# A recommendation tower on one core: layer 1 in 6 chunks of rows in place of 8, with 28 pairs placed by small DMAs

## The chip, the cores and the metric

The kernel runs on one core of a Trainium2 chip. The metric is device time in microseconds (us) of one launch; it is taken as the median of several runs. A profile of one execution shows what each engine did: PE is TensorE, DVE is VectorE, ACT is ScalarE, POOL is GpSimd, SP is the engine that issues most of the DMAs.

## The reference

For 512 samples, 32 fields are looked up in 32 tables of 1000 to 12500 rows of 256 floats. The products of all pairs of fields i < j of a sample, with 16 dense values behind them, go through three layers.

```python
e = jnp.stack([tbl_0[ids[:, 0]], ..., tbl_31[ids[:, 31]]], axis=1)   # [512, 32, 256]
dots = jnp.einsum('bnd,bmd->bnm', e, e)
z = dots[:, iu, ju]                                                  # i < j: [512, 496]
h = jnp.concatenate([z, dense_ctx], axis=1)                          # [512, 512]
h = jnp.maximum(h @ W_top1 + b_top1, 0.0)                            # 512 wide
h = jnp.maximum(h @ W_top2 + b_top2, 0.0)                            # 256 wide
y = h @ W_top3                                                       # 1 wide
```

All of it is in float32.

## The kernel before

*Fields and samples.* Six fields with small tables are looked up by products with one-hot matrices on TensorE (the first third of the span), and the other 26 fields are gathered from HBM by indirect DMAs that POOL issues. There are 104 gathers, numbered 0 to 103, each of 128 rows (4 fields of 32 samples, or the last two fields of 64 samples). They go into a ring `rows` of 14 places; a gather waits until the gather 14 before it has been transposed (`transposed`), and for a point in the products (`dots_half_done`). Nothing else holds them.

*Fills.* TensorE transposes the gathered rows into one of three banks `xt_ps` (L580); that is a fill, of one or two gathers, and there are 57, numbered 0 to 56. ACT or DVE copies a fill into `xt` (L461 and L375; every third one from number 20 on, and number 56, are DVE's). Fill 38 is gather 71 alone. Fill 48 is gathers 89 and 90, fill 52 is gather 97, fills 53 and 54 are gathers 98 to 101, fill 55 is gather 102 and fill 56 is gather 103.

*Batches and rounds.* The 512 samples are 16 batches of 32, and four blocks of 128 (four batches each). `dots` (L608) computes the 32 x 32 products of a batch in 64 TensorE instructions into one of two banks. TensorE's order is written out by hand. After the lookups come rounds 0 to 14: round r computes the products of batch r, then the pieces of the layers that tables assign to the round (`LAYER2_IN`, `LAYER3_IN`, `LAYER1_IN`), then the fills of the round (`FILLS_IN`). Fill 48 is the last of round 12, fill 52 the last of round 13, and rounds 13 and 14 begin with products that need the fills of the round before. Round 14 has fills 53 to 56, and batch 15 comes behind it.

*Moves.* The products lie in a bank as four groups `s` of 32 partitions (row i of the products), with the samples and the column j in the free dimension. Layer 1 wants them with the rows of its contraction on 128 partitions. So `moves` (L255) copies for each `s` four quarters of 8 columns: columns 8q to 8q + 7 go to partitions 32q to 32q + 31 of `pairs`, whose chunk index is the column within the quarter. In quarter 0, chunk 0 would be column 0, which has no pair; the 16 dense values and the bias row lie there, loaded by `load_dense` (L284, on SP). DVE moves three of the four groups (L393), ACT one (L479), and two each in the last two batches. A move of a batch is thus 12 instructions on DVE and 4 on ACT, or 8 and 8.

*Layer 1.* For blocks 0 to 2, `layer1` (L614) contracts 8 chunks of 128 rows with `w1_sb`, for four groups of 128 outputs. `LAYER1_IN` splits the 8 half groups of a block over rounds. One product of 128x128x128 in float32 is two TensorE instructions in the profile, so a half group is 8 instructions and a block is 64. The last block is done per batch, to shorten the end: `flip(m)` (L641) computes the layer for the 32 samples of batch 12 + m with `pairs` as the weights (8 chunks x 4 quarters, 64 instructions), ACT or DVE copies it (`copy_flipped`), `turn(m)` (L651) transposes it, and `relu_turned` puts it into `h1`. Layer 2 is `layer2` (L668), layer 3 is L676.

*The end before.* In round 14, behind fill 54, stand flip 0, layer 2 of block 2, flip 1, turn 0, then fills 55 and 56, the products of batch 15, flips 2 and 3, layer 3 of block 2, turns 1 to 3, layer 2 and layer 3 of block 3, and the store of `y`. DVE applies the second relu of block 2 between its move of batch 14 and its copy of flip 1.

Of the kernel before, what the change touches and what calls it, by code (L numbers as in the profile page):

```python
# [13 lines left out]
P = 128  # L14
# [21 lines left out]
AT_ONCE = 2  # L36
JJ = N_FIELDS // QUADS
KEEP = 8
# [27 lines left out]
LAYER1_IN = {5: (0, [0, 1, 2]), 6: (0, [3, 4, 5]), 7: (0, [6, 7]), 9: (1, [0, 1, 2]), 10: (1, [3, 4, 5]),  # L66
             11: (1, [6, 7]), 12: (2, [0, 1]), 13: (2, [2, 3, 4]), 14: (2, [5, 6, 7])}
RELU1_IN = {7: 0, 11: 1, 14: 2}
# [7 lines left out]
def build_tower(nc, table, first_ids, ids, small_tables, small_ids, dense, w1, w2, b2, w3, out):  # L76
# [14 lines left out]
    with ExitStack() as ctx:  # L91
        def sb(name, shape, dt=F32):
            return ctx.enter_context(nc.sbuf_tensor(name, shape, dt))
# [25 lines left out]
        xt = sb("xt", [P, KEEP, DC, SAMPLES, N_FIELDS])  # L119
        pairs = sb("pairs", [P, 2, JJ, BLOCK])  # L120
        w1_sb = sb("w1_sb", [P, JJ, H1])
# [24 lines left out]
        small_ids_in = [sem(f"small_ids_in{k}") for k in range(TABLE_IDS)]  # L146
        no_pairs_zeroed = sem("no_pairs_zeroed")
        dense_in = [sem(f"dense_in{n}") for n in range(2)]
        w1_in = sem("w1_in")
# [101 lines left out]
        def round_of(f):  # L251

            return next(r for r in range(ROUNDS) if f in fills_in(r))

        def moves(n, s):  # L255

            b, at = divmod(n * SAMPLES, BLOCK)
            for q in range(QUADS):

                skip = int(q == 0)  # L260
                to = pairs[Q * q:Q * (q + 1), b % 2, skip:, at + s * GROUPS:at + (s + 1) * GROUPS]
                column = s % AT_ONCE * Q + q * JJ
                source = dots_ps[n % 2][Q * s:Q * (s + 1), :, column + skip:column + JJ]
                yield to, source.rearrange("i g j -> i j g")

# [15 lines left out]
        def _(sp):  # L281
            sp.dma_start(first_sb[:], first_ids).then_inc(first_ids_in, 16)

            def load_dense(b):  # L284
                sp.dma_start(pairs[0:dense.shape[0], b % 2, 0, :],
                             dense[:, b * BLOCK:(b + 1) * BLOCK]).then_inc(dense_in[b % 2], 16)
# [31 lines left out]
            sp.dma_start(w2_sb[:], w2).then_inc(w2_in, 16)  # L318
            for b in range(2, NB):

                sp.wait_ge(l1_done, N1 * (b - 1))
                load_dense(b)
            sp.wait_ge(y_ready, NB)
# [26 lines left out]
        def _(dve):  # L350

            nc.vector.memset(pairs[0:Q, :, 0, :], 0.0).then_inc(no_pairs_zeroed, 1)
            dve.wait_ge(first_ids_in, 16)
# [32 lines left out]
            def move(n):  # L386
                dve.wait_ge(dots_done, n + 1)
                if n % BATCHES == 0 and n // BATCHES >= 2:

                    dve.wait_ge(l1_done, N1 * (n // BATCHES - 1))  # L390
                for s in dve_quads(n):
                    for to, source in moves(n, s):
                        done = nc.vector.tensor_copy(to, source)  # L393
                done.then_inc(moved_dve, 1)
# [40 lines left out]
        def _(act):  # L435
# [36 lines left out]
            def move(n):  # L472
                act.wait_ge(dots_done, n + 1)
                if n % BATCHES == 0 and n // BATCHES >= 2:

                    act.wait_ge(l1_done, N1 * (n // BATCHES - 1))
                for s in act_quads(n):
# [38 lines left out]
            for r in range(ROUNDS):  # L516
# [11 lines left out]
                for f in fills_in(r):  # L528
# [15 lines left out]
        def _(pe):  # L544
# [67 lines left out]
            def layer1(b, n, columns, to):  # L612
                for j in columns:
                    done = nc.tensor.matmul(to, w1_sb[:, j, n * P:(n + 1) * P], pairs[:, b % 2, j, :],  # L614
                                            start=(j == 0), stop=(j == JJ - 1))
                if columns[-1] == JJ - 1:
                    done.then_inc(l1_done, 1)

            def pairs_complete(b):
                pe.wait_ge(moved_dve, BATCHES * (b + 1))  # L620
                pe.wait_ge(moved_act, BATCHES * (b + 1))
                pe.wait_ge(dense_in[b % 2], 16 * (b // 2 + 1))

            def flip(m):

                b = NB - 1
                moved = BATCHES * b + m + 1
                pe.wait_ge(moved_dve, moved)
                pe.wait_ge(moved_act, moved)
                if m == 0:  # L630
                    pe.wait_ge(dense_in[b % 2], 16 * (b // 2 + 1))

                    pe.wait_ge(h1_ready, b - 1)
                elif m == 1:
                    pe.wait_ge(h1_ready, b)
                elif m == 2:

                    pe.wait_ge(last_h1_act, 1)
                for j in range(JJ):
                    for q in range(QUADS):  # L640
                        done = nc.tensor.matmul(flip_ps[m][Q * q:Q * (q + 1), :],  # L641
                                                pairs[:, b % 2, j, m * SAMPLES:(m + 1) * SAMPLES],
                                                w1_sb[:, j, q * P:(q + 1) * P], start=(j == 0), stop=(j == JJ - 1))
                done.then_inc(flip_done, 1)
# [56 lines left out]
            for r in range(ROUNDS):  # L701
# [22 lines left out]
            layer3(NB - 2, l3_ps)  # L724
            for m in range(1, BATCHES):
                turn(m)

# [74 lines left out]
```

## Time and profile before

| | |
|---|---|
| median of three runs | 162.0 us (161.57 to 162.75) |
| profiled execution, its own time | 162.26 us |
| its span, first to last instruction | 160.5 us |
| granted TensorE clock, mean | 1.000 |
| busy: PE, weight loads, POOL, DVE, ACT | 148.6, 130.2, 104.0, 89.1, 73.0 us |
| instructions | 4781 |

The span is what the profile can divide; 1.76 us of the execution's time lie outside it. A busy TensorE is one with matmuls in flight, which overlap: an instruction of layer 1 is listed with 279 ns and one follows the other every 120 ns.

### The profile page before, as it was taken

How to read it: one execution, taken by the hardware profiler on the slowest of the kernel's cores; microseconds unless marked ns; L12 is line 12 of the kernel's file. 1: busy time of each engine (PE TensorE's matmuls, PEld its weight loads, DVE VectorE, ACT ScalarE, POOL GpSimd, SP SyncE). 2: the span in 40 equal slices, each digit the busy share in tenths (PEclk: the TensorE clock that was granted, in tenths of full speed). 3: DMA queues.
4: the chain of work that ended last, by engine and by line, in shares of the span. 5: the costliest groups of instructions: out<-in, count | busy, mean ns of one | idle time of the engine just before them, and what ended most of it. 6: DMA issues, size and time to landing. Idle time of an engine off the chain costs nothing.

```text
span 160.5 us, 4781 instructions
## 1 busy us (share of the span) xinstructions
PE 148.6 (93%) x1974; PEld 130.2 (81%) x1974; DVE 89.1 (56%) x287; ACT 73.0 (45%) x178; POOL 104.0 (65%) x110
## 2 busy tenths in 40 slices
PE   6999999899999989988989999799989798998994
PEld 6788888788868868777869989699979797997972
DVE  0799976746847034998708644708554344353410
ACT  3356787484764336564340543603441505071421
POOL 1587777777878777777777777777777777700000
PEclk9999999999999999999999999999999999999999
DMA  4899989778655756953333433343333333310000
GB/s 122 239 346 361 371 286 285 206 242 223 186 164 183 204 192 228 267 162 107 102 98 112 118 104 102 101 117 110 103 101 108 115 111 98 102 35 4 4 0 5
DMA packets 11423, 24.58 MB, mean 153 GB/s; under 512 B 2757, under 2 KB 3209, under 8 KB 11402
## 3 DMA queue, kind: packets, MB, share of 16 engines
q0 software_dynamic: 4992, 13.64, 29.2%
q1 hardware_dynamic: 6266, 10.38, 19.9%
q8 instruction: 16, 0.26, 0.6%
q10 hardware_dynamic: 144, 0.26, 0.6%
q14 instruction: 5, 0.04, 0.1%
HBM read 24.26 MB, written 0.00 MB: 151 GB/s over the span
## 4 chain that ended last, share of the span: by engine, by line
PE 40%; POOL 32%; issue 15%; DMA 9%; ACT 3%; DVE 0%; POOLq 0%
POOL rows L345 32%; PE bank L614 11%; PE bank L608 11%; DMA rows<-table,row_ids 6%; PE bank L641 5%; PE xt_ps L580 5%; PE bank L560 3%; PE bank L668 2%; DMA first_sb<-first_ids 2%; ACT xt L461 1%; PE xt_ps L668 1%; PE bank L676 1%; ACT h L495 0%; PE xt_ps L676 0%; ACT h L487 0%
## 5 line engine op out<-in xcount | busy, mean ns | idle before, releaser
L345 POOL DMA_INDIRECT rows<-table,row_ids x104 | 103.4, 994 | 35.0 <-issue 29.0
L393 DVE COPY pairs<-bank 32x64 f32<-32x64 f32 (+1 forms) x184 | 39.6, 215 | 6.7 <-PE bank L608 2.2
L461 ACT COPY xt<-xt_ps 128x512 f32<-128x512 f32 (+1 forms) x44 | 23.0, 557 | 36.3 <-PE xt_ps L580 35.8
L608 PE MATMUL bank<-xt 128*64 128x64 f32 x1024 | 33.4, 223 | 3.6 <-ACT xt L461 2.5
L608 PEld LDWEIGHTS bank<-xt 128*64 128x64 f32 x1024 | 31.3, 138 | 6.5 <-ACT xt L461 3.7
L580 PE MATMUL xt_ps<-ident,rows 128*128 128x128 f32 x208 | 29.6, 277 | 4.1 <-DMA rows<-table,row_ids 3.9
L580 PEld LDWEIGHTS xt_ps<-ident,rows 128*128 128x128 f32 x208 | 23.1, 140 | 8.5 <-DMA rows<-table,row_ids 4.2
L364 DVE TENSOR_SCALAR one_hot<-small_ids_sb,first_sb 128x512 fp32r<-128x512 int32 x48 | 22.2, 493 | 10.1 <-PE bank L560 10.1
L560 PE MATMUL bank<-one_hot,high 128*128 128x512 f32 x96 | 26.5, 398 | 0.0
L375 DVE COPY xt<-xt_ps 128x512 f32<-128x512 f32 (+1 forms) x13 | 8.2, 630 | 32.2 <-PE xt_ps L580 32.2
L560 PE MATMUL bank<-one_hot,low 128*128 128x512 f32 x96 | 25.8, 391 | 0.0
L614 PE MATMUL bank<-pairs,w_sb 128*128 128x128 f32 x192 | 23.7, 279 | 0.0
L614 PEld LDWEIGHTS bank<-pairs,w_sb 128*128 128x128 f32 x192 | 22.1, 192 | 0.9 <-issue 0.4
L560 PEld LDWEIGHTS bank<-one_hot,low 128*128 128x128 f32 x96 | 17.9, 188 | 4.0 <-DVE low L369 0.3
L560 PEld LDWEIGHTS bank<-one_hot,high 128*128 128x128 f32 x96 | 17.4, 188 | 3.8 <-DVE one_hot L364 0.4
L369 DVE TENSOR_TENSOR low<-small_sb,high 128x512 fp32r<-128x512 f32 x24 | 16.4, 683 | 0.4 <-ACT high L449 0.2
L449 ACT CAST high<-small_sb 128x512 fp32r<-128x512 f32 x23 | 13.9, 634 | 5.4 <-DMA small_sb<-small_tables 5.3
L456 ACT COPY kept<-bank 128x512 f32<-128x512 f32 x11 | 11.6, 1161 | 10.2 <-PE bank L560 10.2
L479 ACT COPY pairs<-bank 32x56 f32<-32x56 f32 (+1 forms) x72 | 14.6, 203 | 3.5 <-PE bank L608 2.5
L641 PE MATMUL bank<-w_sb,pairs 128*32 128x128 f32 x256 | 7.8, 274 | 0.0
L641 PEld LDWEIGHTS bank<-w_sb,pairs 128*32 128x32 f32 x256 | 6.7, 110 | 0.6 <-DVE pairs L393 0.3
L668 PE MATMUL bank<-h,w_sb 128*128 128x128 f32 x48 | 6.2, 281 | 0.0
(37 smaller groups left out, 41.3 us busy)
## 6 DMA issues: line engine op xcount, KB each, us to landing
small_sb<-small_tables SPq DMA_DIRECT2D x23, 256.0 KB, 5.1
w_sb<-w SPq DMA_DIRECT2D x8, 256.0 KB
rows<-table,row_ids POOLq DMA_INDIRECT x104, 3.7
small_ids_sb<-small_ids SPq DMA_DIRECT2D x5, 256.0 KB, 5.8
w_sb<-w SPq DMA_DIRECT2D x1, 512.0 KB, 5.9
small_ids_sb<-small_ids ACTq DMA_DIRECT2D x1, 256.0 KB, 3.7
small_sb<-small_tables SPq DMA_DIRECT2D x2, 128.0 KB, 3.5
ids_sb<-ids SPq DMA_DIRECT2D x1, 100.0 KB, 3.2
```

What stands on the lines that cost most here:

```text
L345: nc.gpsimd.indirect_dma_start(rows[:, i % ROWS, :], None, table, bass.IndirectOffsetOnAxis(ap=row_ids[:, i:i + 1], axis=0)).then_inc(gath ...
L364: nc.vector.tensor_scalar(one_hot[:, i % ONE_HOTS, :], small_ids_sb[:, k % TABLE_IDS, :], chunk_rows_sb[:, c:c + 1], None, ALU.is_equal).t ...
L369: nc.vector.tensor_tensor(low[:, k, c - 1:c + 1, :], small_sb[:, k, c - 1:c + 1, :], high[:, k, c - 1:c + 1, :], ALU.subtract).then_inc(lo ...
L393: done = nc.vector.tensor_copy(to, source)
L449: nc.scalar.copy(high[:, k, c:c + 2, :], small_sb[:, k, c:c + 2, :]).then_inc(high_ready, 1)
L461: nc.scalar.copy(*fill_parts(f)).then_inc(xt_act, 1)
L479: done = nc.scalar.copy(to, source)
L560: last = nc.tensor.matmul(banks[FOUND_BANKS[k][d]][:], part[:, k % TABLES, c, d * P:(d + 1) * P], one_hot[:, i % ONE_HOTS, :], start=(c == ...
L580: last = nc.tensor.transpose(to, rows[:, i % ROWS, c * P:(c + 1) * P], ident[:])
L608: done = nc.tensor.matmul(dots_ps[n % 2][quads, g, :], x, x, start=(c == 0), stop=(c == DC - 1))
L614: done = nc.tensor.matmul(to, w1_sb[:, j, n * P:(n + 1) * P], pairs[:, b % 2, j, :], start=(j == 0), stop=(j == JJ - 1))
L641: done = nc.tensor.matmul(flip_ps[m][Q * q:Q * (q + 1), :], pairs[:, b % 2, j, m * SAMPLES:(m + 1) * SAMPLES], w1_sb[:, j, q * P:(q + 1) * ...
```

## The change

Columns 0 to 7 are no longer a quarter of their own. The 24 columns 8 to 31 make four quarters of 6, so `pairs` has 6 chunks in place of 8 (`JJ`), and `w1_sb` too: 48 instructions of layer 1 for a block in place of 64, 48 for a flip in place of 64. Quarter 0 holds columns 8 to 13, whose pairs i < j need rows 0 to 12 only, and 14 rows are kept for them (`OWN_ROWS`). The 28 pairs of the first 8 fields (columns 1 to 7) go to rows 14 to 21 and 22 to 29 of quarter 0, which are free: `side_move` copies 14 rows x 13 columns (1 to 13) x 8 samples of each group in one instruction to `pairs`, 7 chunks of which (`SIDE`) are only a place to put them down, and then two DMAs from SP carry the columns 1 to 5 and 6 to 7 from partitions 0 to 7 to their rows. For blocks 0 to 2 that is one pair of DMAs for a block, for the last block one pair for a batch. Layer 1 of a block and each flip wait for them.

The number of copies stays 4 for each group: one of 14 partitions x 104 elements and three of 32 x 48, in place of one of 32 x 56 and three of 32 x 64. All side moves of a batch stand ahead of its other moves, on DVE and on ACT.

The order changes too: layer 1 of block 2 is done in rounds 13 and 14 (4 half groups of 6 instructions each) and not in round 12 any more; layer 2 of block 2 goes from between flips 0 and 1 to between flips 2 and 3, with turn 1 behind it; DVE's second relu of block 2 goes behind its copy of flip 2; ACT's relu of turn 1 goes ahead of its copy of flip 3. The zeroing at the start covers 32 x 1536 elements in place of 32 x 256, and SP loads 6 chunks of layer 1's weights in place of 8. The weights are laid out for it on the host.

```diff
+FIRST = 8
+SIDE = FIRST - 1
+JJ = (N_FIELDS - FIRST) // QUADS
+OWN_ROWS = FIRST + JJ
+
+SIDE_PLACES = (OWN_ROWS, 0, JJ - 1), (OWN_ROWS + FIRST, JJ - 1, SIDE)
-JJ = N_FIELDS // QUADS
...
-             11: (1, [6, 7]), 12: (2, [0, 1]), 13: (2, [2, 3, 4]), 14: (2, [5, 6, 7])}
+             11: (1, [6, 7]), 13: (2, [0, 1, 2, 3]), 14: (2, [4, 5, 6, 7])}
...
-        pairs = sb("pairs", [P, 2, JJ, BLOCK])
+        pairs = sb("pairs", [P, 2, SIDE + JJ, BLOCK])
+        own_pairs = pairs[:, :, SIDE:, :]
...
+        def side_move(n, s):
+            half, samples = places(n, s)
+            return pairs[0:OWN_ROWS, half, :, samples], source_of(n, s, OWN_ROWS, 1, SIDE + JJ)
+
         def moves(n, s):
-            b, at = divmod(n * SAMPLES, BLOCK)
-            for q in range(QUADS):
-                skip = int(q == 0)
-                to = pairs[Q * q:Q * (q + 1), b % 2, skip:, at + s * GROUPS:at + (s + 1) * GROUPS]
-                column = s % AT_ONCE * Q + q * JJ
-                source = dots_ps[n % 2][Q * s:Q * (s + 1), :, column + skip:column + JJ]
-                yield to, source.rearrange("i g j -> i j g")
+            half, samples = places(n, s)
+            for q in range(1, QUADS):
+                yield own_pairs[Q * q:Q * (q + 1), half, :, samples], source_of(n, s, Q, FIRST + q * JJ, JJ)
...
-            for b in range(2, NB):
-                sp.wait_ge(l1_done, N1 * (b - 1))
-                load_dense(b)
+            def place_sides(b, samples, into):
+                for row, first, last in SIDE_PLACES:
+                    sp.dma_start(own_pairs[row:row + FIRST, b % 2, 1:1 + last - first, samples],
+                                 pairs[0:FIRST, b % 2, first:last, samples]).then_inc(into, 16)
+            for b in range(NB):
+                if b >= 2:
+                    sp.wait_ge(l1_done, N1 * (b - 1))
+                    load_dense(b)
+                if b < NB - 1:
+                    sp.wait_ge(sides_moved_act, BATCHES * (b + 1))
+                    sp.wait_ge(sides_moved_dve, BATCHES * (b + 1))
+                    place_sides(b, slice(0, BLOCK), sides_in[b])
+            for m in range(BATCHES):
+                sp.wait_ge(sides_moved_act, BATCHES * (NB - 1) + m + 1)
+                sp.wait_ge(sides_moved_dve, BATCHES * (NB - 1) + m + 1)
+                place_sides(NB - 1, slice(m * SAMPLES, (m + 1) * SAMPLES), last_sides_in[m])
...
-            nc.vector.memset(pairs[0:Q, :, 0, :], 0.0).then_inc(no_pairs_zeroed, 1)
+            nc.vector.memset(own_pairs[0:Q], 0.0).then_inc(no_pairs_zeroed, 1)
...
+                for s in dve_quads(n):
+                    done = nc.vector.tensor_copy(*side_move(n, s))
+                done.then_inc(sides_moved_dve, 1)
...
                         move(NM - 2)
-                        dve.wait_ge(biases_in, 32)
-                        dve.wait_ge(l2_done, (NB - 1) * N2)
-                        for k in range(N2):
-                            nc.vector.tensor_scalar(h2[:, k, :], l2_ps[k], b2_sb[:, k:k + 1], 0.0,
-                                                    ALU.add, ALU.max).then_inc(h2_ready, 1)
                         copy_flipped(1)
...
             copy_flipped(2)
+            dve.wait_ge(biases_in, 32)
+            dve.wait_ge(l2_done, (NB - 1) * N2)
+            for k in range(N2):
+                nc.vector.tensor_scalar(h2[:, k, :], l2_ps[k], b2_sb[:, k:k + 1], 0.0,
+                                        ALU.add, ALU.max).then_inc(h2_ready, 1)
...
             move(NM - 1)
+            relu_turned(1)
             copy_flipped(3)
             keep_y(NB - 2, l3_ps)
-            relu_turned(1)
             relu_turned(3)
...
             def pairs_complete(b):
...
+                pe.wait_ge(sides_in[b], 16 * len(SIDE_PLACES))
             def flip(m):
...
+                pe.wait_ge(last_sides_in[m], 16 * len(SIDE_PLACES))
...
                         flip(0)
-                        layer2_of(NB - 2)
                         flip(1)
                         turn(0)
                     fill(f)
             for half in (2 * NM - 2, 2 * NM - 1):
                 dots(half)
             flip(2)
+            layer2_of(NB - 2)
+            turn(1)
             flip(3)
             layer3(NB - 2, l3_ps)
-            for m in range(1, BATCHES):
-                turn(m)
+            turn(2)
+            turn(3)
```

ACT has the same loop of side moves, with `sides_moved_act`, ahead of its own moves.

## Rows read from the trace of the kernel before

**Rows 1.** The page: busy time of PE and POOL, and the chain by line.
```profile
PE 148.6 (93%) x1974; PEld 130.2 (81%) x1974; DVE 89.1 (56%) x287; ACT 73.0 (45%) x178; POOL 104.0 (65%) x110
...
POOL rows L345 32%; PE bank L614 11%; PE bank L608 11%; DMA rows<-table,row_ids 6%; PE bank L641 5%; PE xt_ps L580 5%; PE bank L560 3%; PE bank L668 2%; DMA first_sb<-first_ids 2%; ACT xt L461 1%; PE xt_ps L668 1%; PE bank L676 1%; ACT h L495 0%; PE xt_ps L676 0%; ACT h L487 0%
```
**Rows 2.** Who waited for whom: POOL's gathers (total us, times, longest us).
```profile
POOL rows L345 <- issue: 29.0, 95, 0.3
```
**Rows 3.** Timeline of POOL: gathers 33, 97 and 103 (start us, us).
```profile
50.85 1.36 POOL L345 DMA_INDIRECT rows<-table,row_ids  x1 [0.30 <-issue]
...
131.39 0.95 POOL L345 DMA_INDIRECT rows<-table,row_ids  x1 [0.30 <-issue]
...
138.89 0.95 POOL L345 DMA_INDIRECT rows<-table,row_ids  x1 [0.30 <-issue]
```
**Rows 4.** The chain in order of time (start us, us, what).
```profile
98.87 2.74 DMA rows<-table,row_ids
...
101.74 0.41 PE xt_ps L580 x2
...
110.46 2.88 PE bank L614 x24
```
**Rows 5.** Timeline of PE, rounds 12 to 14 and the end.
```profile
123.76 1.95 PE L614 MATMUL bank<-pairs,w_sb 128*128 128x128 f32 x16
...
127.86 2.08 PE L608 MATMUL bank<-xt 128*64 128x64 f32 x64 [0.83 <-ACT xt L461]
...
133.18 1.71 PE L580 MATMUL xt_ps<-ident,rows 128*128 128x128 f32 x14
135.48 2.08 PE L608 MATMUL bank<-xt 128*64 128x64 f32 x64 [0.59 <-ACT xt L461]
...
141.25 1.96 PE L641 MATMUL bank<-w_sb,pairs 128*32 128x128 f32 x64
143.13 2.05 PE L668 MATMUL bank<-h,w_sb 128*128 128x128 f32 x16
...
147.16 0.60 PE L580 MATMUL xt_ps<-ident,rows 128*128 128x128 f32 x4
148.33 2.09 PE L608 MATMUL bank<-xt 128*64 128x64 f32 x64 [0.56 <-ACT xt L461]
150.34 3.93 PE L641 MATMUL bank<-w_sb,pairs 128*32 128x128 f32 x128
...
155.53 2.05 PE L668 MATMUL xt_ps<-h,w_sb 128*128 128x128 f32 x16 [0.37 <-ACT h L495]
```
**Rows 6.** Groups by line and shape: the moves and the zeroing.
```profile
L393 DVE COPY pairs<-bank 32x64 f32<-32x64 f32 x138 | 30.2, 219 | 1.9
...
L479 ACT COPY pairs<-bank 32x64 f32<-32x64 f32 x54 | 11.1, 205 | 0.6
L393 DVE COPY pairs<-bank 32x56 f32<-32x56 f32 x46 | 9.4, 204 | 4.9 <-PE bank L608 2.2 <-issue 2.2
...
L352 DVE MEMSET pairs<- 32x256 f32 x1 | 0.3, 272 | 0.8 <-PEq L796 0.8
```
**Rows 7.** SP's dense loads (ns min/median/max, first and last start); packets in 118.5 to 120.5; SP's timeline.
```profile
L285 SPq DMA_DIRECT2D pairs<-dense x4: 246/247/356, 8.4 to 118.7; - x4
...
q1 hardware_dynamic: 18, 0.01, 1.5%
...
158.94 0.24 SPq L324 DMA_DIRECT2D out<-y  x1
```
**Rows 8.** What SP waited for at the end (total us, times, longest us).
```profile
SPq L91 <- DMA out<-y: 0.9, 1, 0.9
```
**Rows 9.** DMA issues by line (KB each, median us from issue to landing).
```profile
first_sb<-first_ids SPq DMA_DIRECT2D x1, 8.0 KB, 3.9
b_sb<-b SPq DMA_DIRECT2D x1, 1.0 KB, 7.1
```
**Rows 10.** Timeline of ACT at the end.
```profile
154.72 0.25 ACT L504 COPY y<-bank 1x128 f32<-1x128 f32 x1
```

More of the change, by code:

```diff
@@ L147, in build_tower @@
         no_pairs_zeroed = sem("no_pairs_zeroed")
+        sides_moved_act = sem("sides_moved_act")
+        sides_moved_dve = sem("sides_moved_dve")
+        sides_in = [sem(f"sides_in{b}") for b in range(NB - 1)]
+        last_sides_in = [sem(f"last_sides_in{m}") for m in range(BATCHES)]
         dense_in = [sem(f"dense_in{n}") for n in range(2)]
@@ L253, in round_of, with source_of, places @@
             return next(r for r in range(ROUNDS) if f in fills_in(r))
-        def moves(n, s):
-            b, at = divmod(n * SAMPLES, BLOCK)
-            for q in range(QUADS):
-                skip = int(q == 0)
-                to = pairs[Q * q:Q * (q + 1), b % 2, skip:, at + s * GROUPS:at + (s + 1) * GROUPS]
-                column = s % AT_ONCE * Q + q * JJ
-                source = dots_ps[n % 2][Q * s:Q * (s + 1), :, column + skip:column + JJ]
-                yield to, source.rearrange("i g j -> i j g")
+        def source_of(n, s, n_rows, column, n_columns):
+            at = s % AT_ONCE * Q + column
+            return dots_ps[n % 2][Q * s:Q * s + n_rows, :, at:at + n_columns].rearrange("i g j -> i j g")
+        def places(n, s):
+            b, at = divmod(n * SAMPLES, BLOCK)
+            return b % 2, slice(at + s * GROUPS, at + (s + 1) * GROUPS)
+        def side_move(n, s):
+            half, samples = places(n, s)
+            return pairs[0:OWN_ROWS, half, :, samples], source_of(n, s, OWN_ROWS, 1, SIDE + JJ)
+        def moves(n, s):
+            half, samples = places(n, s)
+            for q in range(1, QUADS):
+                yield own_pairs[Q * q:Q * (q + 1), half, :, samples], source_of(n, s, Q, FIRST + q * JJ, JJ)
         def turned_parts(m):
@@ L284, in load_dense @@
             def load_dense(b):
-                sp.dma_start(pairs[0:dense.shape[0], b % 2, 0, :],
+                sp.dma_start(own_pairs[OWN_ROWS:OWN_ROWS + dense.shape[0], b % 2, 0, :],
                              dense[:, b * BLOCK:(b + 1) * BLOCK]).then_inc(dense_in[b % 2], 16)
@@ L476, in move @@
                     act.wait_ge(l1_done, N1 * (n // BATCHES - 1))
+                for s in act_quads(n):
+                    done = nc.scalar.copy(*side_move(n, s))
+                done.then_inc(sides_moved_act, 1)
                 for s in act_quads(n):
@@ L613, in layer1 @@
                 for j in columns:
-                    done = nc.tensor.matmul(to, w1_sb[:, j, n * P:(n + 1) * P], pairs[:, b % 2, j, :],
+                    done = nc.tensor.matmul(to, w1_sb[:, j, n * P:(n + 1) * P], own_pairs[:, b % 2, j, :],
                                             start=(j == 0), stop=(j == JJ - 1))
@@ L641, in flip @@
                         done = nc.tensor.matmul(flip_ps[m][Q * q:Q * (q + 1), :],
-                                                pairs[:, b % 2, j, m * SAMPLES:(m + 1) * SAMPLES],
+                                                own_pairs[:, b % 2, j, m * SAMPLES:(m + 1) * SAMPLES],
                                                 w1_sb[:, j, q * P:(q + 1) * P], start=(j == 0), stop=(j == JJ - 1))
@@ L777 @@
     w1 = np.zeros((QUADS, Q, JJ, H1), W1.dtype)
-    w1[j // JJ, i, j % JJ] = W1[row_of[np.array(order)[i], np.array(order)[j]]]
-    w1[0, 0:dense.shape[1], 0] = W1[len(iu):]
-    w1[0, dense.shape[1], 0] = a["b_top1"]
+    own = j >= FIRST
+    of_pair = W1[row_of[np.array(order)[i], np.array(order)[j]]]
+    w1[(j[own] - FIRST) // JJ, i[own], (j[own] - FIRST) % JJ] = of_pair[own]
+    for row, first, last in SIDE_PLACES:
+        here = (j > first) & (j <= last)
+        w1[0, row + i[here], j[here] - first] = of_pair[here]
+    w1[0, OWN_ROWS:OWN_ROWS + dense.shape[1], 0] = W1[len(iu):]
+    w1[0, OWN_ROWS + dense.shape[1], 0] = a["b_top1"]
     arrays = {
```

## The prediction

> **What bounds the kernel now.** I read the page first: TensorE is busy 93% of the span, POOL 65%, and the chain gives POOL's gathers 32% [rows 1]. A reader would take the first number for the bound and credit the whole saving on TensorE. The second view, who waited for whom, speaks against that: of POOL's idle time 29.0 us are 95 gaps of 0.3 us with nothing waited for [rows 2]. POOL's timeline shows what that means: between gather 97 (131.39) and gather 103 (138.89) lie six steps of 1.25 us, 0.95 of the instruction and 0.30 of the gap [rows 3]. So POOL issues without a stop, and its pace does not depend on TensorE. The third view, the chain in order of time, shows how the two meet: gather 71 starts at 98.87 and lands 2.74 later, at 101.61; its two transposes end at 102.15, and TensorE had waited for it [rows 4]. From 102 on TensorE does not wait for a landing any more and runs behind the gathers, which is why the chain runs on TensorE to the end. How far behind it runs is what decides here. Gather 97, the last that round 13 needs, lands at 131.39 + 2.74 = 134.13; its transposes end at 133.18 + 1.71 = 134.89 and cannot end before 134.13 + 0.54 = 134.67 (0.54 as for gather 71 [rows 4]). So at the start of round 14, at 135.48 [rows 5], TensorE is only 0.2 us behind. Everything it saves ahead of that beyond 0.2 us turns into waiting; what it saves behind it, in the last 25 us, counts.
>
> **1. Six chunks in blocks 0 to 2.** A piece of 24 instructions takes 2.88 us [rows 4], 0.12 each. A block loses 16 of 64, 1.92 us, and three blocks 5.8 us. From round 9 on that is 0.72 + 0.72 + 0.48 in rounds 9 to 11, and 1.9 more in round 12, which loses its 16 instructions (123.76 [rows 5]); rounds 13 and 14 keep 24 each. Together 3.8 us. Followed round by round against landings 1.25 us apart: in round 10 TensorE catches up with gather 81 (114.1), in round 12 with gather 90 (125.4; its transposes would end at 125.9, DVE's copy of fill 48 and the step to TensorE take some 0.8, so round 13 starts at 126.7 in place of 127.86 [rows 5]), and in round 13 with gather 97. Round 14 starts at 134.67 + 0.59 (ACT's copy of fill 52 [rows 5]) = 135.25 in place of 135.48. Sum: -0.25 us. The other 3.55 us, and all of blocks 0 and 1 before round 9, are waiting for gathers. Since POOL does not stop today, it gains nothing from a faster TensorE either.
>
> **2. Six chunks in the flips.** 128 instructions take 3.93 us, 64 take 1.9 [rows 5]. Each flip loses a quarter, 0.48 us; four lose 1.9 us. All four lie behind 135.48 with no landing ahead of them: the last gather lands at 138.89 + 2.74 = 141.6 [rows 3, 4], and fills 55 and 56, now at 147.16 [rows 5], would be reached near 144.0. -1.9 us.
>
> **3. Layer 2 of block 2** moves from 143.13 to behind flip 2: 1.98 us come forward and are paid later, 0. It is now what TensorE does while the last pairs are placed. Its relu on DVE comes behind copy 2 (copy 2 near 149.4, layer 2's end at 150.6, relus to 151.3), and layer 3 of block 2 stands behind flip 3 (152.2), so nobody waits for it. Ahead of fills 55 and 56 ACT must have moved batch 14 and copied flip 0: it starts when layer 1 is done (140.2) and needs 0.6 + 0.5 + 1.7 + 0.3, until 143.3, before flip 1 ends at 143.9. This cover is 0.6 us thick; without it each further tenth would cost a tenth.
>
> **4. Turn 1 and ACT's order.** Turn 1 and its relu leave the stretch behind flip 3. Before, flip 3 ends at 154.27 (150.34 + 3.93), ACT keeps y at 154.72 [rows 10], applies two relus, and layer 2 starts at 155.53 [rows 5], 1.26 later. With one relu of some 0.25 less, bounded by the turns that remain, I take -0.15 (between 0 and -0.25).
>
> **5. The moves.** The shapes' rows give 219 ns for 64 elements and 204 for 56 on DVE, 205 on ACT for 64 [rows 6]: a slope of 1.9 ns an element at most. A side move has 104 elements, so 0.26 to 0.30 us on DVE; the three of 48 elements give back 16 elements each, and the sum of elements is the same, 248. A batch costs what it cost, 0. But the order matters: the side moves come first, two on each engine, and are through 0.6 us after the products.
>
> **6. The small DMAs.** For blocks 0 to 2 they are issued a round before layer 1 of the block (batch 11's side moves in round 12 near 120, use in round 13 near 129), hidden whatever a row here gives. SP's queue: the dense loads of blocks 2 and 3 stand between them and wait for layer 1 of blocks 0 and 1, which is done 4 and more us ahead of what stands behind; the output waits anyway. For flip 2 the side moves are done near 142.3, the use is at 147.2. For flip 3 it is tight. The products of batch 15 end at 147.2 (150.41 less 3.2, from parts 1 to 3), the side moves at 147.8; SP issues two DMAs of 0.25 us [rows 7], the second from 148.1. TensorE does flip 2 (1.44), layer 2 (1.98) and turn 1 (0.16) and is at flip 3 at 150.8, and the other moves end at 149.1. So the second DMA may take 2.7 us from its issue. No row shows a copy from SBUF to SBUF, nor its 40 packets of 128 bytes. Bounds: the store of y is issued at 158.94, and SP waits for it 0.9 us behind its 0.24 of issue [rows 7, 8], 1.2 us; the dense load of 17 rows, issued at 118.7, has all 18 packets in by 120.5 beside the gathers [rows 7], under 1.8 us; the load of the first ids, 128 rows at a cold start, takes 3.9 us [rows 9]. I take 1.8, the nearest in rows and packets: landed by 149.9, hidden by 0.9 us. At 1.2 it is hidden too; at 3.9 flip 3 waits until 152.0, +1.2 us.
>
> The Trainium skill ("DMA: Bandwidth & Descriptors", section on the anatomy of one DMA) puts the fixed cost of a DMA issued by GpSimd at about 2.0 us, almost all of it the wait for the write's receipt; by it as an estimate flip 3 would still find its rows, with 0.7 us to spare in place of 0.9. The same page asks for at least 512 bytes a packet ("Specifications"), and says further on that copies within SBUF are spared the penalty of small packets; no row of this trace shows which holds for 128 bytes.
>
> **7. The rest.** The zeroing grows from 256 to 1536 elements; if all of its 272 ns [rows 6] scaled, it would take 1.6 us, from 0.8 to 2.4, and DVE waits for the first ids until 4.6 us (0.74 + 3.9 [rows 9]). 0. One more wait for each flip and block on TensorE: between 0 and 0.05 each, +0.1 in all. Two loads of weights less: 0.
>
> **Sum.** -0.25 - 1.9 + 0 - 0.15 + 0.1 = -2.2 us. The profiled execution took 162.26 (span 160.5 and 1.76 around it); that makes a span of 158.3 and a time of 160.1. The median of the runs is 0.26 lower; I forecast 159.9, 1.3% under the median. About 1% is what a measurement of this kernel can tell from no change, a line at 160.4.
>
> **Rivals.** *A: flip 3 waits for its rows.* For it speaks that such a DMA has many more packets than the store, that two are issued in turn, and the 3.9 us row; against it that the dense load beside the gathers was in within 1.8. It gives +0.3 to +1.2, 160.2 to 161.1; I name it at 160.9. *B: the same wait, much longer.* The load of the second bias, 1 KB in packets of 8 bytes, took 7.1 us [rows 9], with large loads around it. If tiny packets are the reason, the rows land at 148.1 + 7.1 = 155.2 in place of the use at 150.8: +4.4 and -2.2, a time of 164.2. The side decides at 2.7 + 2.2 = 4.9 us for a DMA; from there on the kernel is slower than before. Against it: DMA engines are idle at that point. *C: the gathers come sooner.* Some gathers take longer than 0.95 (gather 33 1.36 [rows 3]), and there are two large loads less around them. Each such 0.4 us saved before gather 97 comes through in full: 159.4. *D: the change doesn't give its quarter.* A flip's time may hang on more than its number of instructions (starts, waits, the copies behind them), or ACT's cover of part 3 is gone; half of the 1.9 is then lost: 161.0. A rival that I give nearly nothing is that all 7.7 us of TensorE come through (154.5): gather 97's landing forbids it.
>
> **How the numbers follow.** Forecast 0.60 (159.3 to 160.5), A 0.19, B 0.05, C 0.08, D 0.08. Both ends of what is unknown in the forecast are small: 0.25 in part 4, 0.1 in part 7, the landing of gather 97 by some tenths. The range of 8 in 10 takes the forecast and C, and A and D but for their upper ends: 159.0 to 161.2. Faster by over 1% (under 160.4): nearly all of the forecast, C, a fifth of A: 0.66. Slower by over 1% (above 163.6): B, 0.05. Within 1%: 0.29.
>
> **What the profile would show.** Round 14's products at 135.2 in the changed kernel, with waits for gathers ahead of it of some 3.5 us more than before, in rounds 10, 12 and 13; POOL's last gather again at 138.9. L641 with 192 instructions and 5.9 us in place of 7.8; fills 55 and 56 near 144.0; the products of batch 15 near 145.2; flip 3 right behind turn 1, near 150.8, with no wait on a DMA; the last layer 2 at 153.3. I am wrong if flip 3 waits for the DMA, if the gathers' last start is not 138.9, or if ACT's work in round 14 is late for turn 0.

## The result, and the profile after

The changed kernel takes 160.28 us (median of 20 runs) against 162.0 (20 runs): a ratio of 0.988, with a 95% interval of 0.986 to 0.990. That is faster by 1.2%, 1.7 us; the forecast was 159.9 in a range of 159.0 to 161.2. Three of its 20 runs (161.85, 163.02 and 774.11 us) lie over 1.5% above the fastest and are left out of the ratio. Its profiled execution took 160.33 us with a span of 158.5.

The page of the changed kernel, in the lines that answer to [rows 1]:

```profile
PE 142.2 (90%) x1862; PEld 123.5 (78%) x1862; DVE 90.7 (57%) x287; ACT 72.9 (46%) x178; POOL 104.4 (66%) x110
...
POOL rows L379 22%; PE bank L600 15%; DMA rows<-table,row_ids 14%; PE bank L648 8%; PE xt_ps L620 6%; PE bank L654 6%; PE bank L683 4%; PE xt_ps L738 3%; PE xt_ps L710 1%; PE bank L710 1%; DVE pairs L430 1%; PE bank L718 1%; PE bank L693 0%; ACT xt L498 0%; DVE xt L409 0%
```

TensorE has 112 instructions less and is busy 6.4 us less, and the span is 2.0 us shorter. In the chain the landing of gathers went from 6% to 14%: more of the time is now spent waiting for rows. The waits say so directly (total us, times, longest us), in the changed kernel and, last, in the kernel before:

```profile
POOL rows L379 <- issue: 28.0, 92, 0.3
...
PE xt_ps L620 <- DMA rows<-table,row_ids: 7.1, 11, 1.2
```
```profile
PE xt_ps L580 <- DMA rows<-table,row_ids: 3.9, 7, 0.9
```

POOL issues as before, with its gaps of 0.3 us [rows 2], and TensorE's waits for landings went from 3.9 us to 7.1. POOL's timeline shows gathers 97 and 103, 0.30 us later than in [rows 3]:

```profile
131.69 0.95 POOL L379 DMA_INDIRECT rows<-table,row_ids  x1 [0.30 <-issue]
...
139.19 0.95 POOL L379 DMA_INDIRECT rows<-table,row_ids  x1 [0.30 <-issue]
```

The timeline of TensorE from the last fill of round 13 to the end, beside [rows 5]:

```profile
134.58 0.41 PE L620 MATMUL xt_ps<-ident,rows 128*128 128x128 f32 x2 [0.35 <-DMA rows<-table,row_ids]
135.45 2.09 PE L648 MATMUL bank<-xt 128*64 128x64 f32 x64 [0.46 <-ACT xt L498]
...
141.22 2.83 PE L683 MATMUL bank<-w_sb,pairs 128*32 128x128 f32 x96
...
144.14 0.60 PE L620 MATMUL xt_ps<-ident,rows 128*128 128x128 f32 x4
145.30 2.08 PE L648 MATMUL bank<-xt 128*64 128x64 f32 x64 [0.56 <-ACT xt L498]
147.32 1.52 PE L683 MATMUL bank<-w_sb,pairs 128*32 128x128 f32 x48
148.76 2.05 PE L710 MATMUL bank<-h,w_sb 128*128 128x128 f32 x16
150.65 0.27 PE L693 MATMUL bank<-ident,flipped 128*128 128x128 f32 x1
150.86 1.52 PE L683 MATMUL bank<-w_sb,pairs 128*32 128x128 f32 x48
...
153.53 2.05 PE L710 MATMUL xt_ps<-h,w_sb 128*128 128x128 f32 x16 [0.37 <-ACT h L535]
```

Read it in two parts. Round 14 starts at 135.45, as before (135.48): ahead of it stands a wait for gather 97. From there to the end of the span the kernel before took 160.5 - 135.48 = 25.02 us, the changed one 158.5 - 135.45 = 23.05. All of the gain, 1.97 us, lies in this last stretch. Flip 3 follows turn 1 with no wait for a DMA in its row (150.86).

The groups by shape, beside [rows 6] (out, in, count, busy us, mean ns):

```profile
L430 DVE COPY pairs<-bank 32x48 f32<-32x48 f32 x138 | 27.9, 202 | 2.2
...
L426 DVE COPY pairs<-bank 14x104 f32<-14x104 f32 x46 | 11.7, 254 | 4.9 <-PE bank L648 4.4
...
L386 DVE MEMSET pairs<- 32x1536 f32 x1 | 1.3, 1338 | 1.1 <-PEq L845 1.1
```

And SP's small DMAs, first the group (ns min/median/max, first and last start us), then the last pair of the timeline and the second of the two by itself:

```profile
L341 SPq DMA_DIRECT2D pairs<-pairs x14: 624/685/762, 74.3 to 148.8; - x14
...
148.03 1.41 SPq L341 DMA_DIRECT2D pairs<-pairs  x2
...
148.75 0.69 SPq L341 DMA_DIRECT2D pairs<-pairs  x1
```

One such DMA holds SP for 0.69 us, where a dense load held it 0.25 [rows 7] (in this kernel 0.42, the median of four). The first of the pair moves 5 KB, 40 packets of 128 bytes, and the second 2 KB, 16 packets; both hold SP for 0.69 us.

### The profile page after: what moved, and what is told of

It is laid out like the page before. It is cut to its first block, busy times and chain, and to the rows that moved or that the text cites. A ratio compares the mean times of both kernels' runs of the same rounds, so it can differ in the third digit from the quotient of the medians.

```text
span 158.5 us, 4579 instructions
## 1 busy us (share of the span) xinstructions
PE 142.2 (90%) x1862; PEld 123.5 (78%) x1862; DVE 90.7 (57%) x287; ACT 72.9 (46%) x178; POOL 104.4 (66%) x110
## 4 chain that ended last, share of the span: by engine, by line
PE 45%; POOL 22%; issue 14%; DMA 14%; DVE 2%; ACT 1%; POOLq 0%
POOL rows L379 22%; PE bank L600 15%; DMA rows<-table,row_ids 14%; PE bank L648 8%; PE xt_ps L620 6%; PE bank L654 6%; PE bank L683 4%; PE xt_ps L738 3%; PE xt_ps L710 1%; PE bank L710 1%; DVE pairs L430 1%; PE bank L718 1%; PE bank L693 0%; ACT xt L498 0%; DVE xt L409 0%
## 5 line engine op out<-in xcount | busy, mean ns | idle before, releaser
L620 PE MATMUL xt_ps<-ident,rows 128*128 128x128 f32 x208 | 30.5, 278 | 7.9 <-DMA rows<-table,row_ids 7.1
L430 DVE COPY pairs<-bank 32x48 f32<-32x48 f32 x138 | 27.9, 202 | 2.2
L654 PE MATMUL bank<-pairs,w_sb 128*128 128x128 f32 x144 | 18.2, 281 | 0.0
L654 PEld LDWEIGHTS bank<-pairs,w_sb 128*128 128x128 f32 x144 | 16.7, 192 | 0.9 <-issue 0.4
L426 DVE COPY pairs<-bank 14x104 f32<-14x104 f32 x46 | 11.7, 254 | 4.9 <-PE bank L648 4.4
L519 ACT COPY pairs<-bank 32x48 f32<-32x48 f32 x54 | 10.3, 192 | 0.8
L683 PE MATMUL bank<-w_sb,pairs 128*32 128x128 f32 x192 | 5.9, 274 | 0.0
```

Source lines behind the costliest of these rows:

```text
L426: done = nc.vector.tensor_copy(*side_move(n, s))
L620: last = nc.tensor.transpose(to, rows[:, i % ROWS, c * P:(c + 1) * P], ident[:])
L683: done = nc.tensor.matmul(flip_ps[m][Q * q:Q * (q + 1), :], own_pairs[:, b % 2, j, m * SAMPLES:(m + 1) * SAMPLES], w1_sb[:, j, q * P:(q + ...
```

## The experiments

Two numbers are read from each profile: when the products of round 14 start, which is where TensorE has had its last wait for a gather, and how long it is from there to the end of the span. The first moves with POOL's stream: gather 97 starts between 130.80 and 132.29 us in the twelve profiles that have all gathers. Counted from that start, it repeats: round 14 begins 3.72 to 3.85 us behind it in nine of the ten profiles of the changed kernel and its variants, and 4.09 and 4.16 us behind it in the two of the kernel before and its reordered form, where TensorE is a little behind the gathers. (The tenth is `flip3_first`, with a late landing; see the last section.) The second number repeats as well: 23.05 us in the changed kernel's first profile and 159.1 - 136.04 = 23.06 in another execution of it. Spans are read to 0.1 us, so a stretch is good to some 0.05.

**1. The rounds' work given back** (`x_rounds`, from the changed kernel):

```diff
             def layer1(b, n, columns, to):
+                if b < 2 and columns[0] == 0:
+                    for j in range(2):
+                        nc.tensor.matmul(to, w1_sb[:, j, n * P:(n + 1) * P], own_pairs[:, b % 2, j, :],
+                                         start=True, stop=True)
                 for j in columns:
```

> The changed kernel, with two more products (start anew, overwritten by the first real one) ahead of each of the 4 output groups of layer 1 of blocks 0 and 1: 16 TensorE instructions more in each block, 32 in all, 3.8 us of TensorE, as many as the kernel before had there. Theory (TensorE waits for gathers in rounds 5 to 13, and the saving there turned into waiting): no change, span 158.2 to 158.9 with the products of round 14 at 135.4 plus or minus 0.3, and TensorE's waits for gathers about 3 us shorter. Rival (TensorE's work is what counts everywhere): +3.8 us, span 162.

Measured: ratio to the kernel before 0.986 (0.978 to 0.993), as the changed kernel. Round 14 in its timeline:

```profile
134.54 0.41 PE L620 MATMUL xt_ps<-ident,rows 128*128 128x128 f32 x2 [0.75 <-DMA rows<-table,row_ids]
135.41 2.09 PE L648 MATMUL bank<-xt 128*64 128x64 f32 x64 [0.46 <-ACT xt L498]
```

The span is 158.5 again, round 14 starts at 135.41, and the stretch behind it is 23.09 us. Its waits for landings are 5.8 us in place of 7.1, less of a drop than the 3 us expected; 0.7 of what is missing is one wait of 1.87 us (1.20 in the changed kernel) ahead of round 5, where no work was given back. 3.8 us of TensorE work in the rounds cost nothing: what the change took away in blocks 0 and 1 was worth nothing. (Block 2's 1.9 us in round 12 were not given back here; experiment 7 puts work there.)

**2. The flips' work given back** (`x_flips`, from the changed kernel):

```diff
+                for j in range(2):
+                    for q in range(QUADS):
+                        nc.tensor.matmul(flip_ps[m][Q * q:Q * (q + 1), :],
+                                         own_pairs[:, b % 2, j, m * SAMPLES:(m + 1) * SAMPLES],
+                                         w1_sb[:, j, q * P:(q + 1) * P], start=True, stop=True)
                 for j in range(JJ):
                     for q in range(QUADS):
```

> The changed kernel, with two more products of each quarter ahead of each flip, overwritten by the real ones: 64 instructions in a flip in place of 48, as before the change. Theory (the gain lies in the flips): +1.9 us from four flips of 0.48 each, less what the small DMAs' cover gains nothing: span 160.4. Rival (a flip's time hangs on its start and its waits, not on its instructions, or the gain came from the order): under +1 us, span 159.3 or less.

Measured: ratio 1.003 (0.999 to 1.007), the whole gain gone. Start of round 14 in its timeline:

```profile
135.25 2.08 PE L648 MATMUL bank<-xt 128*64 128x64 f32 x64 [0.46 <-ACT xt L498]
```

The span is 160.1, so the stretch is 24.85 us, 1.80 more than 23.05. In the timeline the four flips are 1.77 us longer, and the products of batch 15 happen to take 0.11 more. The flips' instructions are the gain.

**3. The order alone** (`reorder_only`, the kernel before with the order of the end of the changed one):

```diff
                         flip(0)
-                        layer2_of(NB - 2)
                         flip(1)
...
             flip(2)
+            layer2_of(NB - 2)
+            turn(1)
             flip(3)
             layer3(NB - 2, l3_ps)
-            for m in range(1, BATCHES):
-                turn(m)
+            turn(2)
+            turn(3)
```

with the moves of DVE's second relu and of ACT's relu of turn 1 as in the change.

> The kernel before with the order of the end alone: layer 2 of block 2 and turn 1 between flips 2 and 3, DVE's second relu behind its copy of flip 2, ACT's relu of turn 1 ahead of its copy of flip 3. 8 chunks, no side moves, no DMAs. Theory: -0.15 us (layer 2 of the last block starts 1.1 behind the end of flip 3 in place of 1.26), span 160.3. Rival (the order itself gives a good part of the 2 us): span under 159.7.

Measured: ratio 0.989 (0.979 to 0.999) from two of its four runs, 159.84 and 160.72 us; the other two took 163.17 and 164.04. The times alone don't separate the order from the whole change, whose ratio is the same, and two of the four spans, 158.0 and 158.8, lie under the rival's 159.7. What speaks against the rival is the stretch from round 14 on, read in one profile. That execution took 163.17 us, 3.2 of it outside its span, so only what lies inside the span is read. In its timeline:

```profile
135.28 2.08 PE L608 MATMUL bank<-xt 128*64 128x64 f32 x64 [0.59 <-ACT xt L461]
...
141.05 3.70 PE L641 MATMUL bank<-w_sb,pairs 128*32 128x128 f32 x128
...
155.10 2.05 PE L668 MATMUL xt_ps<-h,w_sb 128*128 128x128 f32 x16 [0.37 <-ACT h L495]
```

The span is 160.0, the stretch 24.72 us, 0.30 less than 25.02. From the products to the last layer 2 it is 19.82 us in place of 20.05: about half of that lies between flip 3 and layer 2, as expected, and the other half where flips 0 and 1 follow each other (141.05 to 144.68 here, 3.63 us, against 1.88 + 1.89 when layer 2 stood between them [rows 5]). The order is worth 0.23 by the timeline and 0.3 by the span, where I took 0.15, and not the larger part.

**4. The gathers out of the way** (`before_half` and `after_half`: the two kernels without every second gather from number 52 on):

```diff
                 for i in fill_gathers(f):
+                    if i >= 52 and i % 2:
+                        continue
...
-                    pe.wait_ge(gathered[i % ROWS], 16 * (i // ROWS + 1))
+                    if i < 52 or i % 2 == 0:
+                        pe.wait_ge(gathered[i % ROWS], 16 * (i // ROWS + 1))
```

> The kernel before, without every second gather from number 52 on (26 of 104 left out, the transposes take whatever the ring holds, so part of the lookup is left out). From round 5 on POOL needs half the time for a round's gathers. Theory (TensorE is only just behind the gathers): its waits for landings after round 5 go, 1.7 us (0.71 at 84.10, 0.16 at 95.34, 0.86 at 101.74), span 158.8. Rival (gathers don't matter from round 5 on): 160.5.

> The changed kernel without the same 26 gathers. Theory: with the gathers out of the way all that the change takes from TensorE comes through, 5.8 us in the rounds and 1.8 in the flips and 0.3 by the order: 7 to 8 us under before_half, span 151 to 152. Rival (something else, as the copies of ACT and DVE or the small DMAs, holds the rounds back as well): 2 to 4 us under before_half.

Measured: 0.980 (0.975 to 0.986) and 0.940 (0.934 to 0.946) of the kernel before; spans 157.2 and 150.2. Start of round 14 in the one and in the other:

```profile
132.25 2.08 PE L611 MATMUL bank<-xt 128*64 128x64 f32 x64 [0.59 <-ACT xt L463]
```
```profile
127.20 2.08 PE L651 MATMUL bank<-xt 128*64 128x64 f32 x64 [0.59 <-ACT xt L500]
```

Without those gathers the change is worth 7.0 us, 5.05 ahead of round 14 and 1.95 behind it (24.95 and 23.0 us). With them it is worth 2.0. The difference, 5 us of the 5.8 that TensorE saves in the rounds, is what the pace of the gathers swallows. The kernel before also got faster by 3.3 us of its span in place of 1.7: TensorE depended on the gathers by more than the rows of its waits after round 5 show. All of that is won by round 9, whose products start at 98.85 in place of 102.08, 3.23 us earlier; round 14 starts 3.23 us earlier too. So from 102 on the kernel before waited for no gather, as the prediction read it.

**5. Flip 3 without its cover** (`flip3_first`, from the changed kernel):

```diff
             flip(2)
-            layer2_of(NB - 2)
-            turn(1)
             flip(3)
+            layer2_of(NB - 2)
+            turn(1)
```

> The changed kernel, with flip 3 right behind flip 2 and layer 2 of block 2 and turn 1 behind both, as in the order before. This takes the cover off the last two small DMAs, so flip 3 starts when they have landed, and measures them. In the changed kernel the second one is issued at 148.8 and its packets are in by 150.2. Theory: flip 3 starts at 150.2 to 150.5 in place of 148.8, TensorE idle 1.4 to 1.7 us, and the span grows by that, to 160.0 (1.8 us from issue as I took it: 150.6, +1.8). Rival (the landing takes the 3.9 us of the first load): this can't be without a wait in the changed kernel, which showed none; the other end, 1.2 us from issue, gives 150.0 and +1.2.

Measured: ratio 1.003 (0.999 to 1.007). Its timeline, the products of batch 15 and what follows:

```profile
146.27 2.09 PE L648 MATMUL bank<-xt 128*64 128x64 f32 x64 [0.56 <-ACT xt L498]
148.28 1.52 PE L683 MATMUL bank<-w_sb,pairs 128*32 128x128 f32 x48
151.57 1.52 PE L683 MATMUL bank<-w_sb,pairs 128*32 128x128 f32 x48 [1.77 <-DMA pairs<-pairs]
...
155.84 0.60 PE L718 MATMUL bank<-h,w_sb 128*1 128x128 f32 x4 [0.66 <-DVE h L463]
```

Flip 3 waits 1.77 us and starts 151.57 - 148.36 = 3.2 us after the end of the products. In the changed kernel's profile these end at 147.38, so the rows were there at 150.6, 0.25 us ahead of flip 3. The second DMA was issued at 148.75: 1.85 us from issue to use, SP's 0.69 included. The span grew by more than the 1.5 us I expected, to 162.1; the stretch from round 14 on is 25.68 us, 2.63 more. 0.66 of it is a wait that I overlooked: with layer 2 this late, layer 3 of block 2 waits for DVE's relu. Another microsecond of the longer span lies ahead of round 14, and the last section comes back to it.

**6. Side moves last** (`sides_last`, from the changed kernel, on DVE and in the same way on ACT; `dots` then waits for the side moves of two batches before):

```diff
-                for s in dve_quads(n):
-                    done = nc.vector.tensor_copy(*side_move(n, s))
-                done.then_inc(sides_moved_dve, 1)
                 for s in dve_quads(n):
                     for to, source in moves(n, s):
                         done = nc.vector.tensor_copy(to, source)
                 done.then_inc(moved_dve, 1)
+                for s in dve_quads(n):
+                    done = nc.vector.tensor_copy(*side_move(n, s))
+                done.then_inc(sides_moved_dve, 1)
```

> The changed kernel with the side moves of every batch behind its other moves on DVE and on ACT (and the next but one products waiting for the side moves in place of the others), so the last small DMAs are issued 1.3 us later. By flip3_first the rows of flip 3 are in 3.2 us after the products of batch 15, 0.25 us ahead of their use in the changed kernel. Theory: flip 3 waits 1.0 us, span +1.0 against the changed kernel. Rival (the cover is 0.9 us thick, as I had predicted): +0.4 us.

Measured: ratio 0.998 (0.993 to 1.003). Its timeline of DVE and TensorE:

```profile
148.60 0.53 DVE L430 COPY pairs<-bank 14x104 f32<-14x104 f32 x2
...
151.79 1.47 PE L683 MATMUL bank<-w_sb,pairs 128*32 128x128 f32 x45 [0.99 <-DMA pairs<-pairs]
```

A wait of 0.99 us, and a stretch of 159.4 - 135.33 = 24.07 us, 1.02 more. So the cover was 0.25 us and not 0.9: two experiments say the same from two sides (here the rows come 2.66 us after the side moves; 147.96 + 2.66 = 150.6 again).

**7. Layer 1 of block 2 spread better** (`v1_one_in_12` and `v2_two_in_12`, from the changed kernel):

```diff
-             11: (1, [6, 7]), 13: (2, [0, 1, 2, 3]), 14: (2, [4, 5, 6, 7])}
+             11: (1, [6, 7]), 12: (2, [0]), 13: (2, [1, 2, 3, 4]), 14: (2, [5, 6, 7])}
```

and for the second `12: (2, [0, 1]), 13: (2, [2, 3, 4, 5]), 14: (2, [6, 7])`. Since the last stretch is what counts and rounds 12 and 13 wait for gathers, layer 1 should leave round 14.

> The changed kernel with block 2's layer 1 spread over three rounds: 1 half group of 6 instructions in round 12, 4 in round 13, 3 in round 14. Theory: round 12 has room for it ahead of gather 90, round 14 gets shorter by 0.72 us and lies behind the last gather that TensorE waits for: -0.7 us, span 157.8. Rival (round 12 is full, so fill 48 and round 13 come later): 0.

> The same with 2 half groups in round 12, 4 in round 13, 2 in round 14. Round 12 waits 0.57 us for gathers and round 13 another 0.54, so 1.44 us come forward and up to 0.3 of it shifts round 13's end: -1.1 to -1.4 us against the changed kernel, span 157.2. With the two half groups in the emptiest stretch, TensorE's clock should also stay at its full level there in every run, where six of twenty runs of the changed kernel show a mean clock under 1. Rival (as above): -0.7 or less.

Both were then run again beside the changed kernel on one chip:

> The changed kernel itself, beside the two spreads below on one chip: ratio to the kernel before 0.988, within 0.003. The mean clock should be 0.989 in about a quarter of the runs, and 1.00 in those of the kernel before.

> Block 2's layer 1 as 1, 4 and 3 half groups over rounds 12 to 14: 0.7 us under after_again (its stretch from round 14 to the end is 22.33 us in the first profile, against 23.05). Rival (the first ratio of 0.975 was right): 2 us under it.

> 2, 4 and 2 half groups: 1.1 us under after_again by the stretch from round 14 on (21.92 us against 23.05); of the 1.44 us that come forward 0.2 went into waiting for gather 103, which is the next bound. Rival (a lower clock takes some of it back, as two of six runs showed 0.989 and 0.951): the same as v1_again or slower.

| | ratio to the kernel before | median, us | round 14 to the end, us |
|---|---|---|---|
| changed kernel | 0.988 (0.986 to 0.990) | 160.28 | 23.05 |
| the same again | 0.989 (0.982 to 0.995) | 160.73 | 23.06 |
| one in round 12 | 0.975 (0.968 to 0.981) | 158.87 | 157.4 - 135.07 = 22.33 |
| the same again | 0.982 (0.976 to 0.988) | 159.36 | 157.0 - 134.62 = 22.38 |
| two in round 12 | 0.980 (0.975 to 0.985) | 158.99 | 156.9 - 134.98 = 21.92 |
| the same again | 0.983 (0.977 to 0.989) | 159.23 | 156.9 - 134.63 = 22.27 |

Both beat both kernels. The one takes 0.7 us out of the last stretch, as expected. Side by side (the runs again) the medians are 1.4 and 1.5 us under the changed kernel's, more than the stretch accounts for; the rest lies ahead of round 14, where gather 97 started at 130.80 and 130.82 against 132.29. One profile of each can't tell whether that is chance. The work put into round 12 cost nothing there: with two half groups round 14 starts 3.80 and 3.81 us behind gather 97's start, against 3.76.

The second takes 0.8 to 1.1 of the 1.44 that left round 14, and its timeline (the run again) shows what is late next:

```profile
141.98 0.38 PE L620 MATMUL xt_ps<-ident,rows 128*128 128x128 f32 x2
142.76 0.41 PE L620 MATMUL xt_ps<-ident,rows 128*128 128x128 f32 x2 [0.40 <-ACT xt L498]
143.74 2.08 PE L648 MATMUL bank<-xt 128*64 128x64 f32 x64 [0.56 <-issue]
```

Fill 55 and fill 56, which were one piece of 0.60 us at 144.14, are 0.4 us apart. The releaser named is ACT's copy, but in the code fill 56 waits only for DVE's copy of fill 53, which ended at 139.85, and for gather 103. That gather started at 138.31; fifteen of its sixteen semaphore events are in the trace by 141.0 and the last one comes at 142.63, 0.13 ahead of fill 56. So the next bound is gather 103, by its last piece. The two spreads can't be told apart by time. Their first ratios (0.975, 0.980) promised more than the second (0.982, 0.983), with intervals that overlap.

## Why the prediction was right

**What bounds the kernel: right.** The claim was that POOL's stream fixes the start of round 14, and that only what is saved behind it counts. Round 14 starts at 135.45 (135.25 forecast, with a stream that was 0.30 us later). From round 9 to round 14 TensorE has 3.84 us less to do and gets there only 0.33 us sooner (33.07 us in place of 33.40), so 3.5 us turned into waiting, as forecast. The rows of the waits don't say it as plainly: in rounds 10, 12 and 13 they name 1.8 us against none before, and the rest of their growth of 3.2 us lies in earlier rounds, so that this sum comes near 3.5 is in part luck. Experiments 1, 2 and 4 show the bound by giving back the one part, giving back the other, and taking the gathers away.

**Part 1, -0.25.** Measured -0.03, or -0.33 if the later stream is taken out. Right within what one profile can tell.

**Part 2, -1.9.** 1.8 by experiment 2. Right in size, but one of its steps held by luck: I let the last gather land at 141.6. It did in the kernel before (141.58), and in the changed kernel's profile gather 103, started at 139.19, landed at 143.93, 4.74 us later. Its fill began at 144.36, so of the 2.4 us that I thought to have there 0.4 were left.

**Parts 3 and 4, 0 and -0.15.** Together -0.23 to -0.30 by experiment 3. Mis-sized by some 0.1: I priced turn 1 and ACT's relu, and not that two flips in a row run 0.14 us shorter than with layer 2 between them. ACT had copied flip 0 at 143.56 (143.3 forecast), 0.4 us ahead of turn 0 at 143.97 where I had 0.6.

**Part 5, the moves.** A side move takes 254 ns on DVE (0.26 to 0.30 forecast, so just under), the others 202; a batch is 2.75 us (119.53 to 122.28) in place of 2.73. Right that a batch costs what it cost.

**Part 6, the small DMAs.** Hidden, as said, and a term of it wrong. I took 1.8 us from issue to landing and measured 1.85 to the use; but I took SP's time to issue one from the dense load, 0.25 us, and it is 0.69. So the second was issued at 148.75 and not at 148.1 (0.47 of that is SP's time, the rest is that the side moves ended at 147.96 and not at 147.8), the rows came at 150.6 and not at 149.9, and of the 0.9 us of cover 0.25 were left. Rival A (flip 3 waits) was closer than its 0.19 said: another 0.3 us of moves ahead of the DMAs, and it would have come. The two DMAs' 1.4 us on SP are the larger half of the 2.6 us from 148.03 to 150.6. I also gave the second DMA 40 packets; it has 16, and the first has 40. B (7 us for tiny packets) is ruled out by the same rows. The Trainium skill's 2.0 us for the fixed cost of a DMA ("DMA: Bandwidth & Descriptors", the anatomy of one DMA) is stated for GpSimd's DMAs; here, for the second of the pair, issued by SP from SBUF to SBUF with 16 packets of 128 bytes, the trace has 1.85, near it.

**Part 7.** The zeroing takes 1.34 us (1.6 forecast), hidden. The waits that the change adds: the stretch with the flips' work given back (24.85) is 0.13 longer than that of the order alone (24.72), where I had 0.1; but 0.1 of it lies in the products of batch 15, which have no new wait, so hardly anything is left for the waits.

**Rivals C and D** didn't show: the stream was later and not earlier in the profile, and the flips gave their quarter. The sum, -2.2 in the profiled execution, came out as -2.0 of span and -1.93 of time (162.26 to 160.33).

## What to carry to other kernels

Where one engine issues a stream without a stop and another works it off, find the last item of the stream on which the other waits: work saved ahead of that point is lost, and work moved there from behind it costs nothing (the changed kernel left half of block 2's layer 1 behind it; moving a fourth or half of that forward gave another 0.5% or more). When a small DMA must hide behind other work, count how long it holds its queue (0.69 us here, with 40 packets and with 16), and not its landing alone. To tell the two halves of a saving apart, give each back by itself as idle work.

## What the runs showed of the hardware

*The clock.* The granted clock fell in stretches of a few microseconds in some executions. In the profile of `flip3_first`, three stretches in turn (length, busy us of PE, PEld, DVE, ACT, POOL with counts, granted clock, DMA share, GB/s): round 12 from its layer 2's end, the products of round 13, and what follows.

```profile
123.05:126.45 3.40, 1.88 (x15) 1.23 (x13) 0.79 (x2) 2.41 (x8) 2.49 (x4) 1.00 0.33 102
126.45:129.89 3.44, 3.44 (x64) 3.33 (x64) 2.39 (x12) 0.00 (x0) 2.55 (x3) 0.53 0.41 116
129.89:133.29 3.40, 3.40 (x31) 3.06 (x30) 0.00 (x0) 0.26 (x1) 2.76 (x3) 0.97 0.39 112
```

The 64 instructions of the products, 2.0 us elsewhere, took 3.44 at a mean of 0.53, that is almost all at the lower level of 1.2 GHz. Ahead of it TensorE was busy 1.88 of 3.40 us. In the changed kernel the same stretches read:

```profile
123.62:127.02 3.40, 1.91 (x15) 1.21 (x13) 0.80 (x2) 2.50 (x8) 2.49 (x4) 1.00 0.34 100
127.02:129.03 2.01, 2.01 (x64) 1.94 (x64) 1.87 (x10) 0.00 (x0) 1.56 (x2) 1.00 0.46 130
```

The same emptiness ahead, 1.91 of 3.40, and the clock stayed. So round 12 is one place where it can fall and doesn't always. In the profile of `v2_two_in_12` it fell elsewhere: the products of round 6 start at 84.34 and take 3.54 us (the granted clock's mean is 0.51 from 86 to 88), and ahead of them TensorE was busy 0.44 of the 2.00 us from 82 to 84. A mean clock of 0.989 or less stood in 5 of 26 runs of the changed kernel, 5 of 10 of `x_flips`, 3 of 10 of `flip3_first`, 3 of 10 of `sides_last`, 2 of 10 of the one-in-12 spread, 2 of 12 of the two-in-12 spread, none of 4 of `x_rounds` and none of 4 of `after_half`, where TensorE waits less; of the kernel before in 2 of 47, one of them a run of 246.53 us at 0.664. That emptier rounds make it more likely fits these counts and isn't shown by them; the one forecast made from it, that two half groups in round 12 keep the clock at its full level there, can't be told from a mean over the whole run, and 2 of 12 runs fell somewhere. In the changed kernel the five runs have spans of 157.3 to 159.7 among 157.3 to 161.2 (and one of 772.3, far outside everything else), so what it costs there can't be told.

*A gather's landing.* In the profile of `flip3_first` gather 97 landed 4.24 us after its start, where it took 2.75 in the changed kernel's; round 14 started at 136.42, though the gather itself had been issued at 131.17. Of its sixteen semaphore events fifteen are in by 133.9; the last comes at 135.41. Gather 103 has such a late last piece in eight of the ten profiles of kernels with 6 chunks and all gathers: it lands 3.69 to 4.90 us after its start there, and 2.7 to 2.8 in the other two and in the two profiles with 8 chunks. Why is open. A kernel that waits for each landing takes such a delay in full when nothing covers it.
